# Layer 0 of a four-layer kernel: eight places instead of four for the routed experts' outputs, straight-line quad loops, and the second half's row sends moved ahead

## The reference

```python
x = L0_attn_x                       # 4096 tokens of 128
xn = _layernorm(x, axis=-1)
x = x + _L0_attn_ref(xn, ...) + _L0_ffn_ref(xn, ...)
...
def _L0_ffn_ref(x, ln_scale, ln_bias, gate_w, Wg, Wu, Wd, sWg, sWu, sWd):
    def _swiglu(x, wg, wu, wd):
        return jax.nn.silu(x @ wg) * (x @ wu) @ wd
    ...
    probs = jax.nn.softmax(logits, axis=-1)
    tk_probs, tk_idx = jax.lax.top_k(probs, 2)
    tk_probs = tk_probs / (jnp.sum(tk_probs, axis=-1, keepdims=True) + EPS)
    ...
    out = _swiglu(xf, sWg, sWu, sWd)
    for e in range(8):
        out = out + w[:, e:e + 1] * _swiglu(xf, Wg[e], Wu[e], Wd[e])
```

## Time and profile before

| what | us |
|---|---|
| median of three runs | 1184.08 |
| lowest and highest run | 1180.83, 1184.82 |
| profiled execution, first to last instruction | 1183.1 |
| PE busy in it | 1009.2 |
| DVE busy in it | 782.2 |
| ACT busy in it | 641.2 |
| POOL busy in it | 383.9 |

### The profile page before, as it was taken

How to read it: one execution, slowest core, us unless ns; L and a number is a source line. 1 busy time by engine, 2 the same in 40 slices (tenths; PEclk the granted TensorE clock), 3 DMA queues, 4 the chain that set the end, 5 groups by cost and what they waited for, 6 DMA issues and landing times. The chain is left out here.

```text
span 1183.1 us, 30904 instructions
## 1 busy us (share of the span) xinstructions
PE 1009.2 (85%) x10716; PEld 604.2 (51%) x10717; DVE 782.2 (66%) x1436; ACT 641.2 (54%) x1144; POOL 383.9 (32%) x542
## 2 busy tenths in 40 slices
PE   5488686999859899979789999999988599999696
PEld 2256576886434455536535554455545255554242
DVE  8844242453668899828767677677775788995345
ACT  4712242443536677753256767766656277777364
POOL 2154577665054555553030000000000155555011
PEclk9689697999878999989889999999999699999698
DMA  9588743542653333342000000000017233331002
GB/s 281 207 261 258 241 112 97 161 137 62 197 191 92 106 108 109 87 144 72 0 1 1 0 0 1 0 0 0 0 59 261 82 88 108 109 111 46 1 1 71
DMA packets 166612, 114.18 MB, mean 97 GB/s; under 512 B 15732, under 2 KB 160383, under 8 KB 166547
## 3 DMA queue, kind: packets, MB, share of 16 engines
q1 hardware_dynamic: 161938, 104.40, 29.4%
q0 software_dynamic: 4608, 8.93, 2.2%
HBM read 77.04 MB, written 37.29 MB: 97 GB/s over the span
## 5 line engine op out<-in xcount | busy, mean ns | idle before, releaser
L1685 ACT ACTIVATE at_p<-banks 128x512 f32<-128x512 f32 x384 | 222.6, 597 | 93.6 <-PE banks L1559 89.9
L1701 DVE TENSOR_REDUCE at_mx<-banks 128x12 f32<-128x1536 f32 x128 | 224.2, 1758 | 44.5 <-PE banks L1544 41.8
L1499 POOL TENSOR_SCALAR_AFFINE_SELECT at_p<-at_p 128x512 f32<-128x512 f32 x256 | 159.3, 634 | 163.3 <-ACT at_p L1685 157.0
L1559 PE MATMUL banks<-at_qbl,at_kst 128*128 128x512 f16 x384 | 143.1, 391 | 1.5 <-ACT at_p L1685 1.5
L1491 POOL COPY at_va<-v_all 128x128 f32 (+1 forms) x64 | 16.8, 292 | 306.3 <-PEq L1518 306.3
L1970 PE MATMUL banks<-f_h_hi,w_hi_h 128*128 128x512 f16 x256 | 97.2, 380 | 6.0 <-DVE f_h L2113 3.2
L1971 PE MATMUL banks<-f_h_lo,w_hi_h 128*128 128x512 f16 x256 | 97.0, 379 | 0.0
L1972 PE MATMUL banks<-f_h_hi,w_lo_h 128*128 128x512 f16 x256 | 97.0, 379 | 0.0
L486 POOL DMA_INDIRECT expert_outs<-ex_x_lo,rows_back_to x80 | 80.0, 1000 | 43.3 <-issue 27.4
L475 POOL DMA_INDIRECT expert_rows<-xn_tok,slot x64 | 65.3, 1020 | 83.9 <-DVE slot L1040 42.6
L1572 PE MATMUL banks<-at_p,at_va 128*32 128x256 f32 x1024 | 81.4, 379 | 0.0
(11 more groups left out here) (417 smaller groups left out, 2333.2 us busy)
## 6 DMA issues: line engine op xcount, KB each, us to landing
xnT<-kernel_padded SPq DMA_DIRECT2D x8, 1024.0 KB, 7.6
at_qst<-at_q_stacked SPq DMA_DIRECT2D x32, 256.0 KB, 3.0
at_ksc<-at_k_stacked SPq DMA_DIRECT2D x32, 256.0 KB, 3.4
at_kst<-at_k_stacked SPq DMA_DIRECT2D x32, 256.0 KB, 2.9
at_qbl<-at_q_stacked SPq DMA_DIRECT2D x128, 64.0 KB, 2.0
expert_rows<-ex_h_sb SPq DMA_DIRECT2D x1, 5760.0 KB, 18.0
gate_up_then_rows<-expert_rows SPq DMA_DIRECT2D x20, 260.0 KB, 3.2
ssm_powers<-kernel_padded SPq DMA_DIRECT2D x4, 1024.0 KB, 6.4
```

The source lines that it names most:

```text
L1499: pool.affine_select(out=blk, in_=blk, compare_op=ALU.is_ge, fill=0.0, base=0, pattern=[[0, 4], [1, P]], channel_multiplier=-1).then_inc(p ...
L1559: pe.matmul(o, kst[m][:, g, kt * P:kt * P + P], qbl[m][:, g, :, qt * P:qt * P + P], start=True, stop=True).then_inc(t_mm, 1)
L1685: act.activation(dst, k.ps[:, turn_bank(old, g * 3 + n), :].rearrange("p (j q) -> p j q", j=4), ACT.Exp, scale=scale).then_inc(p_ready, 1)
L1701: dve.tensor_reduce(mx[:, :, g * 4:g * 4 + 4].rearrange("p n j -> p j n"), k.ps[:, score_banks(batch, g), 0:3 * P].rearrange("p j (n t) -> ...
```

## The change

The ring gets eight places. Places 0 to 3 of `ysc` stay where they are. Places 4 to 7 lie in `powers_then_toeplitz` (trace name `ssm_powers`), which the convolution has done with by then. The rings for loaded rows (XR) and for the turned rows stay at four and two. All eight groups of second-half row sends are issued before the first outputs. The loops over quads on POOL, ACT and DVE are written out; PE's stays. In the counted waits nothing changes but the ring's size: a place is awaited from quad 8 on.

```diff
-XR, YR = 4, 4
+XR, YR = 4, 8
...
-    ysc = xl[:].bitcast(F32).rearrange("p (m b c) -> p m b c", m=YR, c=DM)
+    ysc = [slots[:, m] for slots in (xl[:].bitcast(F32).rearrange("p (m b c) -> p m b c", m=YR // 2, c=DM),
+                                     powers_then_toeplitz[:].rearrange("p (m b c) -> p m b c", m=YR // 2, c=DM))
+           for m in range(YR // 2)]
...
-            def send_outs(quad):
-                a, r = quad
-                pool.wait_ge(ids_done, a * 4 + r + 1)
-                pool.wait_ge(out_copied, a * 4 + r + 3)
+            def send_outs(q):
+                r = q % YR
+                pool.wait_ge(ids_done, q + 1)
+                pool.wait_ge(out_copied, q + 3)
...
-            for group in range(GROUPS - 4):
+            for group in range(8):
                 send_rows(1, group)
-            for r in range(4):
-                send_outs((0, r))
-                send_rows(1, GROUPS - 4 + r)
-            with pool.Fori(0, QUADS // 4 - 1) as j:
-                for r in range(4):
-                    send_outs((j + 1, r))
+            for q in range(QUADS):
+                send_outs(q)
+                if 8 + q < GROUPS:
+                    send_rows(1, 8 + q)
...
-            def copy_out(quad):
-                a, r = quad
-                act.wait_ge(down_mm, a * 4 + NCH + r + 3)
-                if not isinstance(a, int) or a:
-                    act.wait_ge(out_sent[r], a * (TPC * 16))
+            def copy_out(q):
+                r = q % YR
+                act.wait_ge(down_mm, NCH + q + 3)
+                if q >= YR:
+                    act.wait_ge(out_sent[r], q // YR * TPC * 16)
...
-            for q in range(5):
-                quad_silus(of_four(q), of_four(q + 1), of_four(q - 1) if q else None)
-            with act.Fori(0, 3) as j:
-                for r in range(4):
-                    quad_silus((j + 1 + (r + 1) // 4, (r + 1) % 4), (j + 1 + (r + 2) // 4, (r + 2) % 4), (j + 1, r))
-            for q in range(17, QUADS):
-                quad_silus(of_four(q), of_four(q + 1) if q + 1 < QUADS else None, of_four(q - 1))
-            copy_out(of_four(QUADS - 1))
+            for q in range(QUADS):
+                silu((NCH + q) * IT, 0)
+                if q + 1 < QUADS:
+                    rows_high(of_four(q + 1))
+                if q:
+                    copy_out(q - 1)
+                silu((NCH + q) * IT + 1, 1)
+            copy_out(QUADS - 1)
...
             def rows_low(quad):
                 a, r = quad
-                dve.wait_ge(q_hi, a * 4 + r + 1)
-                if not isinstance(a, int) or a:
-                    dve.wait_ge(out_sent[r], a * (TPC * 16))
+                q = a * 4 + r
+                dve.wait_ge(q_hi, q + 1)
+                if q >= YR:
+                    dve.wait_ge(out_sent[q % YR], q // YR * TPC * 16)
                 dve.tensor_tensor(xql[:, r % 2], k.ps[:, ROWS_B, :], xqh[:, r % 2], ALU.subtract).then_inc(q_lo, 1)
-                dve.tensor_copy(row_weight[:, r, :], xg[:, r, :, DM + 1])
-                dve.tensor_copy(ids[:, r, :], xg[:, r, :, DM]).then_inc(ids_done, 1)
+                dve.tensor_copy(row_weight[:, q % YR, :], xg[:, r, :, DM + 1])
+                dve.tensor_copy(ids[:, q % YR, :], xg[:, r, :, DM]).then_inc(ids_done, 1)
```

More of the change, by code:

```diff
@@ L486, in send_outs @@
                     pool.indirect_dma_start(rows_out, bass.IndirectOffsetOnAxis(ap=ids[:, r, b:b + 1], axis=0),
-                                            ysc[:, r, b, :], None, bounds_check=2 * TOKENS - 1,
+                                            ysc[r][:, b, :], None, bounds_check=2 * TOKENS - 1,
                                             oob_is_err=False).then_inc(out_sent[r], 16)
@@ L598, in rows_high @@
                 act.activation(xqh[:, r % 2], k.ps[:, ROWS_B, :], ACT.Copy).then_inc(q_hi, 1)
-            def copy_out(quad):
-                a, r = quad
-                act.wait_ge(down_mm, a * 4 + NCH + r + 3)
-                if not isinstance(a, int) or a:
-                    act.wait_ge(out_sent[r], a * (TPC * 16))
+            def copy_out(q):
[3 more added lines that the diff above has]
+                    act.wait_ge(out_sent[r], q // YR * TPC * 16)
                 for b in range(TPC):
-                    ins = act.activation(ysc[:, r, b, :], k.ps[:, OB[r % 2], b * P:b * P + P], ACT.Copy,
+                    ins = act.activation(ysc[r][:, b, :], k.ps[:, OB[q % 2], b * P:b * P + P], ACT.Copy,
                                          scale=row_weight[:, r, b:b + 1])
                 ins.then_inc(out_copied, 1)
[L610 to L617, removed]
-            rows_high((0, 0))
-            for q in range(5):
-                quad_silus(of_four(q), of_four(q + 1), of_four(q - 1) if q else None)
-            with act.Fori(0, 3) as j:
-                for r in range(4):
-                    quad_silus((j + 1 + (r + 1) // 4, (r + 1) % 4), (j + 1 + (r + 2) // 4, (r + 2) % 4), (j + 1, r))
-            for q in range(17, QUADS):
-                quad_silus(of_four(q), of_four(q + 1) if q + 1 < QUADS else None, of_four(q - 1))
-            copy_out(of_four(QUADS - 1))
+            rows_high((0, 0))
+            for q in range(QUADS):
[6 more added lines that the diff above has]
+            copy_out(QUADS - 1)
             for c in range(NCH):
@@ L1187, in _ @@
             gated(0, 1, NCH * IT + 1, None)
[L1188 to L1195, removed]
-                    if r % 2:
-                        residual((j + 1, r // 2))
-                        add_out((j + 1, r // 2))
-            for q in range(17, QUADS):
+            for q in range(1, QUADS):
                 quad_gated(of_four(q), of_four(q + 1) if q + 1 < QUADS else None)
+                if q % 2 == 0 and q // 2 <= NCH:
+                    residual(of_two(q // 2 - 1))
+                    add_out(of_two(q // 2 - 1))
             for c in range(NCH):
```

## The result

The changed kernel took 1171.06 us in the median of five runs (1163.95 to 1172.69), against 1184.08 for the kernel before (five runs, 1179.66 to 1188.05). The ratio is 0.9871, with a 95% interval of 0.9844 to 0.9898, which is 12 to 18 us less. The profiled execution was the quickest of the five and has a span of 1162.0 us, 21.1 under that of the kernel before. The forecast of 1165.8 was 5.3 us too low for this median. The stated range of 1161.5 to 1171.7 holds it by 0.6 us, while the forecast's own narrower one, 1163 to 1170, does not. The forecast gain of 18.3 us, a ratio of 0.9845, lies just inside the interval.

What follows compares the result with a forecast made beforehand. POOL was taken to bound 160 to 210 us through the ring of four, PE after about 215. Stalls 18.3 us, loops and row loads 0, backlog 0 to 1: 1165.8 us forecast, range 1161.5 to 1171.7.

Steps and rivals of the forecast that it cites:

- What bounds the stretch: Layer 0, 160 to 210 us: POOL is the bound, through the ring of four; from about 215 us it is PE.
- The stalls that go: Quads 4 to 8 no longer wait for output DMAs; the stage gains 18.3 us if nothing else is late.
- term of 18.27 us: ACT's output copies: quads 3 to 8 take 50.80 us, quads 9 to 14 take 32.53; the difference is the gain.
- split into 12.5 of idle time and 5.8 of lower clock: Of the 18.27 us, 12.5 is PE idling and 5.8 is PE's work at the lower clock.
- rival of 1171.6: PE's clock stays mixed in 174 to 209 us, so only 12.5 us of waiting is won; chance 0.05.
- POOL's new order: Outputs start at 165.5 instead of 149.28, POOL catches up 1.3 us per quad, and the last starts at 270.2.
- the cap: POOL's sends limit the stage: POOL alone could not end before 269.1, so at most 20.4 us is gained.
- the stretched sends: POOL's sends beside DVE's residual additions run 0.2 to 0.35 us longer per chunk, some 2.4 us over seven chunks.
- The rival from the skill: DVE's additions hold POOL's sends in full, 9.7 us instead of 2.4; gain 11.0, time 1173.1; chance 0.08.
- The ring of eight, the rows of the second half, the loops: Nothing waits for the larger ring; quad 10's row load costs nothing; written-out loops cost zero, within 1 us.
- the margin that was put at 10 us: Quad 0's outputs land by about 174; DVE's low half of quad 8 needs them at about 184.
- The end: The load of the second half's outputs moves with the last output; the work after it is the same.

Runs made afterwards that it cites:

- pe_kept_busy: The kernel before with PE's loop written out and overwritten matmuls (14, 8, 22) on PE before quads 6, 7 and 8: 1180.56 us, ratio 0.9971.
- pool_late: The changed kernel with eight memsets on POOL between the last row send and the first output: 1173.81 us, ratio 0.9881 to the kernel before.
- ring_only: The changed kernel with POOL's old order of sends, keeping the ring of eight and the written-out loops: 1172.85 us, ratio 0.9884 to the kernel before.

## Why the prediction was right

**What bounds the stretch.** That it is POOL, through the ring of four, was right: the ring alone brings 13 us, and filling PE's idle time without it brings nothing.

**The stalls that go.** The term of 18.27 us, from two stretches of equal shape, was measured as 50.80 - 32.77 = 18.0 on the same copies, and 17.7 to 18.2 us on the whole stage in three traces. Its split into 12.5 of idle time and 5.8 of lower clock is the step that does not hold. It is a true account of what PE did in those 50 us, but it reads as two costs. POOL's sends set the length of the stretch, and pe_kept_busy shows that no more than about 1.1 to 1.7 us, behind the last wait, can be the clock's. The sum did not hang on the split. The rival of 1171.6 did ("the idle time goes, but the clock does not come back"), and the first median of 1171.06 looks like it. The traces tell them apart: the clock was 1.00 from 150 to 265 us, and the stage alone gained 18.2. That the first median still fell into the range, 0.6 us from its edge, was partly luck.

**POOL's new order.** The first output was forecast for 165.5 and came at 167.04, 165.66 and 165.32 in the three traces. The last was forecast for 270.2 and came at 269.84, 271.03 and 271.02. One term of the cap, the stretched sends, was put at 2.4 us in all. It differs from execution to execution: over their median of 0.98 us the 80 sends lost 0.6, 0.7 and 2.1 us in the three traces and 0.7 in pool_late. So 2.4 was at the upper end, and POOL was a little ahead of PE rather than just level with it: beyond its usual gaps it stood idle for 0.3, 2.8 and 1.7 us in the three traces. In the first, where it began 1.5 us late, hardly any slack was left.

**The rival from the skill.** The Trainium skill, "SBUF — State Buffer", section "Who interferes with whom", has the later of two contending instructions blocked until the first is over. The traces agree with that. The 9.7 us of the rival did not come all the same, since they price the rule too high. DVE's two additions for a chunk both have two inputs in SBUF. The first pair of rows has a send of 1.42 us that began 0.13 into an addition, the second pair a send that began 0.02 before one:

```profile
230.24 0.69 DVE L1081 TENSOR_TENSOR x_res<-x_res,xn_tok 128x512 f32<-128x512 f32 x1
230.37 1.42 POOL L488 DMA_INDIRECT expert_outs<-ssm_powers,rows_back_to  x1 [0.30 <-issue]
...
205.82 0.98 POOL L488 DMA_INDIRECT expert_outs<-ssm_powers,rows_back_to  x1 [0.31 <-issue]
205.84 0.70 DVE L1084 TENSOR_TENSOR x_res<-x_res,gate_second 128x512 f32<-128x512 f32 x1
```

When the send began, 0.56 of the addition were left, and it took 0.44 longer than 0.98. In all fourteen traces 84 output sends began while such an addition was under way, and each took longer by what was left of it, less 0.12 us (by nothing, where less than that was left), to within 0.01. Four more began at most 0.04 us after the addition and kept their 0.98, while the addition took 0.73 to 0.76 in place of 0.69. No send over 1.03 us was without such an addition. A send thus can lose only the rest of one addition, 0.52 us at most here, and only when it comes second. The rival charged every send with a whole addition. The same section of the Trainium skill takes it as inferred that an addition of this kind (`tensor_tensor`) leaves the issuing of DMAs on GpSimd alone; for these indirect DMAs the traces show otherwise.

**The ring of eight, the rows of the second half, the loops.** No low half waited for an output, and the margin that was put at 10 us agrees with what the smaller rings show: six places, which ask for the outputs two quads sooner, waited about 1 us. Quad 10's rows did no harm even when their load began at 195.27, in ring_only. The loops that the change wrote out cost nothing that can be measured. PE's own, which it left alone, costs 2 to 3 us.

**The end.** The stage's gain reached the end. The forecast took the median of before plus the stage's difference, and did not say that layers 1 and 3 alone scatter by 7 us each over the fourteen traces. A comparison of five runs with five could therefore give 13 or 21 as well as 18. The first one gave 13.0 in the medians and 21.1 in the profiled spans.

## What to carry to other kernels

When an engine runs without a pause and others wait for its results through a ring of buffers, price the stall by the whole stretch, against an unstalled one of the same shape. Between such waits, an idle time or a lower clock on the engine that waits is a symptom, and curing it alone gained nothing here. Work moved ahead of that engine's results is only free if the ring reaches over the delay: here the order without the ring gave 5 us, the ring without the order 13, both 18. Try the ring's size on both sides, since six places did as well as eight and five lost 7 us.

## What the runs showed of the hardware

Indirect DMAs from POOL kept a pitch of 1.29 to 1.30 us over 80 in a row (pool_late, with no wait between), so a long unbroken row of them did not slow down. A send that began while DVE ran an addition with both inputs in SBUF took its own 0.98 us and what was left of the addition, less 0.12 (or its own 0.98 alone, where less than 0.12 was left); 84 sends agree with that to 0.01 us.

TensorE's clock fell to its lower level (0.50 in the rows shown) during or right behind single idle times of 4.2, 6.7 and 10.9 us. With 6.7 of idle time the stage lost 7.3 us, and with 10.9 it lost 12.5, that is 0.6 and 1.6 us beyond the idle time. Between the four waits of the kernel before, which POOL bound, the lower clock cost nothing that can be measured. With idle times of at most 2.2 us (pe_kept_busy) the clock still fell in part, to 0.66 in 205 to 210 us.
